# Threshold sums from absolute differences and a key-sum column, and scores in four row tiles, in a sparsemax attention and mixture-of-experts kernel

## The reference

```
x = x + attention(layernorm(x), ctx)        # 16 heads of width 16, 77 keys
x = x + ffn(layernorm(x))                   # top 2 of 8 experts, and one shared expert

scores = (q @ Wq + bq) . (ctx @ Wk + bk) / 4
attn   = max(scores - tau, 0)               # sparsemax: tau such that each row of 77 sums to 1
out    = attn @ (ctx @ Wv + bv);  out @ Wo + bo

hidden = square(relu(x @ w1[e]));  expert = hidden @ w2[e]      # e = 0..7, and the shared one
ffn    = sum over the two picked experts of weight * expert + shared
```

## Time and profile before

| | |
|---|---|
| median of 3 runs | 917.6 us (917.48 to 919.5) |
| the profiled execution | 916.7 us, span 914.9 us, mean granted clock 0.957 |
| busy, share of the span | PE 801.5 us (88%), DVE 593.5 (65%), ACT 571.3 (62%), POOL 538.3 (59%) |
| chain that ended last, by engine | PE 45%, ACT 22%, issue 15%, DVE 9%, POOL 5%, DMA 3% |
| HBM traffic | 36 GB/s over the span |

### The profile page before, as it was taken

How to read it: one execution, slowest core, us unless ns; L and a number is a source line. 1 busy time by engine, 2 the same in 40 slices (tenths; PEclk the granted TensorE clock), 3 DMA queues, 4 the chain that set the end, 5 groups by cost and what they waited for, 6 DMA issues and landing times.

```text
span 914.9 us, 14519 instructions
## 1 busy us (share of the span) xinstructions
PE 801.5 (88%) x4800; PEld 656.7 (72%) x4800; DVE 593.5 (65%) x1691; ACT 571.3 (62%) x890; POOL 538.3 (59%) x622
## 2 busy tenths in 40 slices
PE   1847657999999999999999999999999999889998
PEld 1535435778777777878777877777787877767887
DVE  2469685867676867768586777786777858642221
ACT  1555667676668676767767666867676776633221
POOL 2447586766667584848686666768484858541010
PEclk9977577999999999999999999999999999989999
DMA  8300101020200202020102020110202010101010
GB/s 253 103 8 1 19 12 47 1 73 6 69 3 25 53 12 59 12 64 14 59 1 72 7 70 1 35 43 12 59 13 64 3 59 1 59 1 59 1 58 11
DMA packets 37355, 34.84 MB, mean 38 GB/s; under 512 B 23153, under 2 KB 34078, under 8 KB 35230
## 3 DMA queue, kind: packets, MB, share of 16 engines
q1 hardware_dynamic: 34934, 28.88, 11.3%
q0 software_dynamic: 1248, 4.73, 1.5%
q10 hardware_dynamic: 1096, 0.29, 0.2%
HBM read 28.30 MB, written 4.33 MB: 36 GB/s over the span
## 4 chain that ended last, share of the span: by engine, by line
PE 45%; ACT 22%; issue 15%; DVE 9%; POOL 5%; DMA 3%; ACTq 0%; POOLq 0%; DVEq 0%
PE y_ps L827 18%; PE h_ps L814 11%; ACT signs L533 10%; ACT hid L584 5%; PE m_ps L778 5%; ACT over L535 4%; PE s_ps L769 4%; POOL over L337 3%; DVE fsum L955 3%; PE m_ps L722 3%; DMA sw_all<-sw_scratch 2%; DVE fold_b L961 2%; ACT xn L481 1%; DVE g L1080 1%; PE m_ps L803 1%
## 5 line engine op out<-in xcount | busy, mean ns | idle before, releaser
L337 POOL TENSOR_TENSOR over<-S,tau 128x1232 f32<-128x1232 f32 x128 | 286.6, 2251 | 232.7 <-DVE tau L973 230.1
L827 PE MATMUL y_ps<-w_sb,hid 128*128 128x256 f32 x1152 | 281.5, 388 | 39.9 <-ACT hid L584 30.2
L814 PE MATMUL h_ps<-x1nT,w_sb 128*128 128x256 f32 x1152 | 275.6, 382 | 0.0
L827 PEld LDWEIGHTS y_ps<-w_sb,hid 128*128 128x128 f32 x1152 | 212.8, 191 | 86.1 <-ACT hid L584 57.7
L814 PEld LDWEIGHTS h_ps<-x1nT,w_sb 128*128 128x128 f32 x1152 | 215.2, 191 | 30.4 <-issue 3.0
L955 DVE TENSOR_REDUCE fsum<-over 128x16 f32<-128x1232 f32 x96 | 137.4, 1431 | 40.7 <-ACT over L535 40.6
L535 ACT ACTIVATE over<-over 128x1232 f32<-128x1232 f32 x128 | 155.6, 1228 | 3.0
L584 ACT ACTIVATE hid<-g 128x512 f32<-128x512 f32 x144 | 89.6, 622 | 65.2 <-DVE g L1080 64.7
L1080 DVE SCALAR_TENSOR_TENSOR g<-h_ps,sw_all 128x512 f32<-128x512 f32 x128 | 87.5, 684 | 58.0 <-PE h_ps L814 36.8
L533 ACT ACTIVATE signs<-over 128x1232 bf16<-128x1232 f32 x96 | 117.1, 1220 | 7.4 <-POOL over L337 7.2
L952 DVE TENSOR_TENSOR fold_a<-signs 128x640 bf16<-128x640 bf16 x96 | 55.7, 580 | 47.2 <-ACT signs L533 47.2
(11 more groups left out here) (104 smaller groups left out, 922.4 us busy)
## 6 DMA issues: line engine op xcount, KB each, us to landing
sw_all<-sw_scratch SPq DMA_DIRECT2D x16, 1024.0 KB, 5.2
x_sb<-in_x SPq DMA_DIRECT2D x16, 256.0 KB, 2.7
w_sb<-in_w POOLq DMA_DIRECT2D x2, 2048.0 KB, 12.1
out_y<-wk_sb SPq DMA_DIRECT2D x16, 256.0 KB, 5.6
sw_all<-in_ctx SPq DMA_DIRECT2D x1, 1078.0 KB
v_block<-v_all SPq DMA_DIRECT2D x56, 9.6 KB
wk_sb<-in_wk SPq DMA_DIRECT2D x1, 256.0 KB
wv_sb<-in_wv SPq DMA_DIRECT2D x1, 256.0 KB
```

The costliest lines, as they stand in the source:

```text
L337: return pool.tensor_tensor(dst, S[:, p, t], tau[:, p, t].rearrange("p (h o) -> p h o", o=1).broadcast_to([P, NH, NK]), ALU.subtract)
L814: last = pe.matmul(h_ps[:, i % 2, c, :], w1_sb[:, e, k, c * P:(c + 1) * P], x1nT[:, p, k, :], start=(k == 0), stop=(k == KC - 1))
L827: last = pe.matmul(y_ps[:, t, :], hid[:, i % 2, c, t * P:(t + 1) * P], w2_sb[:, e, c, :], start=(i == 0 and t == 0 and c == 0), stop=(i == ...
```

## The change: what it does

- ACT no longer rectifies `over` in rounds 0 to 2. DVE sums |S − tau| there (`apply_absolute_value`), and 2f = sum of |S − tau| + sum of (S − tau). The second sum is the sum of the row of S less 77 tau (`lean`, one operation on 128x32). The row's sum comes from PE: `kT` gets a 78th column with the sum of the keys (`key_sums`, a DVE reduction for each pair of elements, eight in all, in turns 0 and 1), and so S gets a 78th column. Round 3 and the attention weights still rectify.
- The order in a round of DVE becomes: `fsum` of a tile as soon as `over` is there, then (tile 1) `lean`, then `fold_a`. The tail is `den`, `step`, reciprocal, multiply, add.
- The check marks rows above and rows below (`below`), on DVE (`mid_verdict`, ahead of `g` 8) instead of POOL; PE counts both with two more matmuls per turn.
- The scores take four row tiles of 32 rows with two heads each: eight matmuls of 156 columns, the fourth row tile into bank 0 of `m_ps`; `k_diag` has two heads per row group instead of four. The wait `s_front` goes. The order of heads in S becomes the plain one, so the table `PLACES` goes.

```diff
-HALF = P // 2
-GH = HALF // DH
-PLACES = (0, 1, 2, 3, 14, 15, 4, 5, 6, 7, 12, 13, 8, 9, 10, 11)
+ROWS = 32
+RT = P // ROWS
+GH = ROWS // DH
+KS = NK + 1
+HALF_KEYS = GH * KS
...
-        kT = sb("kT", [P, KC, NB, NK])
-        k_diag = sb("k_diag", [P, KC, GH, NK])
+        kT = sb("kT", [P, KC, NB, KS])
+        k_diag = sb("k_diag", [P, KC, GH, KS])
...
-                pool.wait_ge(k_taken.sem, k_taken.at(b // 2))
+                pool.wait_ge(keys_summed.sem, keys_summed.at(b // 2))
...
-                flat = S[:, p, t].rearrange("p h k -> p (h k)")
-                act.activation(flat[:, 0:12 * NK].rearrange("p (a n) -> p a n", a=2), s_ps[:, 0:2, 0:6 * NK],
+                slots = S[:, p, t].rearrange("p (c r j) k -> p r c (j k)", c=KC, j=GH)
+                act.activation(slots[:, 0:SB], s_ps[:, :, 0:KC * HALF_KEYS].rearrange("p r (c n) -> p r c n", c=KC),
                                ACT.Copy, scale=DH ** -0.5)
-                act.activation(flat[:, 12 * NK:], s_ps[:, 2, 0:4 * NK], ACT.Copy, scale=DH ** -0.5
-                               ).then_inc(s_taken.sem, 1)
+                act.activation(slots[:, SB], m_ps[:, 0, 0:KC * HALF_KEYS].rearrange("p (c n) -> p c n", c=KC),
+                               ACT.Copy, scale=DH ** -0.5).then_inc(s_taken.sem, 1)
...
                     act.activation(signs[:, p, t, :, 0:NK], over[:, p, t], ACT.Sign).then_inc(sign_done.sem, 1)
-                    act.wait_ge(sign_done.sem, sign_done.at(b, rt(r, t)))
-                act.activation(over[:, p, t], over[:, p, t], ACT.Relu).then_inc(relu_done.sem, 1)
+                else:
+                    act.activation(over[:, p, t], over[:, p, t], ACT.Relu).then_inc(relu_done.sem, 1)
...
+                for c in range(KC):
+                    for r in range(RT):
+                        rows = slice(r * ROWS, (r + 1) * ROWS)
+                        bank = s_ps[:, r] if r < SB else m_ps[:, 0]
+                        last = pe.matmul(bank[:, c * HALF_KEYS:(c + 1) * HALF_KEYS], qT[rows, c, t * P:(t + 1) * P],
+                                         k_diag[rows, c].rearrange("p h k -> p (h k)"), start=True, stop=True)
...
+            def key_sums(i):
+                dve.wait_ge(k_taken.sem, k_taken.at(i))
+                dve.tensor_reduce(kT[:, :, 2 * i:2 * i + 2, NK], kT[:, :, 2 * i:2 * i + 2, 0:NK], AX.X, ALU.add
+                                  ).then_inc(keys_summed.sem, 1)
...
+                for t in range(T):
+                    dve.wait_ge(over_ready.sem, over_ready.at(b, rt(r, t)))
+                    dve.tensor_reduce(fsum[:, t * NH:(t + 1) * NH], over[:, p, t], AX.X, ALU.add,
+                                      apply_absolute_value=True).then_inc(f_summed.sem, 1)
+                    if t:
...
+                        dve.scalar_tensor_tensor(lean[:], flat(tau[:, p]), -float(NK), key_totals, ALU.mult, ALU.add
+                                                 ).then_inc(leaned.sem, 1)
+                    elif gap is not None:
+                        gap()
                     dve.wait_ge(sign_done.sem, sign_done.at(b, rt(r, t)))
                     dve.tensor_tensor(fold_a[:, t], signs[:, p, t, :, 0:SW // 2], signs[:, p, t, :, SW // 2:], ALU.add
                                       ).then_inc(signs_folded.sem, 1)
-                    dve.wait_ge(relu_done.sem, relu_done.at(b, rt(r, t)))
-                    dve.tensor_reduce(fsum[:, t * NH:(t + 1) * NH], over[:, p, t], AX.X, ALU.add
-                                      ).then_inc(f_summed.sem, 1)
-                    if gap is not None and t == 0:
-                        gap()
...
                 dve.tensor_reduce(den[:, p], fold_b[:], AX.X, ALU.add).then_inc(newton_chain.sem, 1)
+                dve.wait_ge(f_summed.sem, f_summed.at(b, rt(r, 1)))
+                dve.wait_ge(leaned.sem, leaned.at(b, r + 1))
+                dve.scalar_tensor_tensor(step[:], fsum[:], -2.0, lean[:], ALU.add, ALU.add
+                                         ).then_inc(newton_chain.sem, 1)
                 dve.wait_ge(newton_chain.sem, newton_chain.at(b, n0 + 2))
                 dve.reciprocal(rden[:], den[:, p]).then_inc(newton_chain.sem, 1)
-                dve.wait_ge(newton_chain.sem, newton_chain.at(b, n0 + 3))
-                dve.scalar_tensor_tensor(step[:], fsum[:], -1.0, rden[:], ALU.add, ALU.mult
-                                         ).then_inc(newton_chain.sem, 1)
                 dve.wait_ge(newton_chain.sem, newton_chain.at(b, n0 + 4))
-                dve.scalar_tensor_tensor(flat(tau[:, p]), step[:], 2.0, flat(tau[:, p]), ALU.mult, ALU.add
-                                         ).then_inc(tau_ready.sem, 1)
+                dve.tensor_tensor(step[:], step[:], rden[:], ALU.mult).then_inc(newton_chain.sem, 1)
+                dve.wait_ge(newton_chain.sem, newton_chain.at(b, n0 + 5))
+                dve.tensor_tensor(flat(tau[:, p]), flat(tau[:, p]), step[:], ALU.add).then_inc(tau_ready.sem, 1)
...
+            def mid_verdict(m):
+                dve.wait_ge(attn_ready.sem, attn_ready.at(m))
+                dve.wait_ge(count_done.sem, count_done.at(m - 1))
+                dve.wait_ge(check_chain.sem, check_chain.at(m, 4))
+                dve.scalar_tensor_tensor(unsettled[:], asum[:], -float(NH), tol_sum[:], ALU.add, ALU.is_gt)
+                dve.scalar_tensor_tensor(below[:], asum[:], float(NH), tol_sum[:], ALU.subtract, ALU.is_gt,
+                                         reverse0=True).then_inc(unsettled_known.sem, 1)
...
                 if late:
                     late_weights(b - 2)
+                if mid:
+                    mid_verdict(b - 1)
                 gates(8)
```

More of the change, by code:

```diff
@@ L120, in xattn_moe_kernel @@
         fold_a, fold_b = sb("fold_a", [P, T, NH, SW // 2], BF16), sb("fold_b", [P, T * NH, SW // 4], BF16)
+        lean = sb("lean", [P, T * NH])
         fsum, den = sb("fsum", [P, T * NH]), sb("den", [P, 2, T * NH])
@@ L125, in xattn_moe_kernel @@
         asum, tol_sum, unsettled = (sb(n, [P, T]) for n in ("asum", "tol_sum", "unsettled"))
+        below = sb("below", [P, T])
         unsettled_count = sb("unsettled_count", [1, 1], I32)
@@ L652, in turn @@
                 if new:
[L653 removed]
+                    sign_or_relu(b, p, 1, 0)
                 square(8)
@@ L732, in new_scores @@
                     pe.wait_ge(aT_taken.sem, aT_taken.at(b - 3))
-                for c, r, h0, n, bank, col in ((0, 0, 0, 4, 0, 0), (0, 1, 0, 4, 1, 0), (1, 0, 0, 4, 2, 0),
-                                               (1, 1, 2, 2, 0, 4), (1, 1, 0, 2, 1, 4)):
-                    rows = slice(r * HALF, (r + 1) * HALF)
-                    if (c, bank) == (1, 0):
-                        pe.wait_ge(s_front.sem, s_front.at(b, t + 1))
-                    last = pe.matmul(s_ps[:, bank, col * NK:(col + n) * NK], qT[rows, c, t * P:(t + 1) * P],
-                                     k_diag[rows, c, h0:h0 + n, :].rearrange("p h k -> p (h k)"),
-                                     start=True, stop=True)
-                    if (c, bank) == (0, 0):
-                        last.then_inc(s_front.sem, 1)
+                for c in range(KC):
[4 more added lines that the diff above has]
+                                         k_diag[rows, c].rearrange("p h k -> p (h k)"), start=True, stop=True)
                 last.then_inc(s_done.sem, 1)
@@ L750, in late_unsettled @@
                 pe.wait_ge(y_ready.sem, y_ready.at(m - 2))
-                for t in range(T):
-                    last = pe.matmul(y_ps[0:1, 0, 0:1], unsettled[:, t:t + 1], ones[:], start=(t == 0),
-                                     stop=(t == T - 1))
+                for side in (unsettled, below):
+                    for t in range(T):
+                        last = pe.matmul(y_ps[0:1, 0, 0:1], side[:, t:t + 1], ones[:],
+                                         start=(side is unsettled and t == 0), stop=(side is below and t == T - 1))
                 last.then_inc(count_done.sem, 1)
@@ L928, in new_tau @@
                 for h in range(NH):
-                    last = dve.max(top8[:, t, h], S[:, p, t, h])
+                    last = dve.max(top8[:, t, h], S[:, p, t, h, 0:NK])
                 last.then_inc(top_chain.sem, 1)
```

71 lines of the change are left out of this document (35 added, 36 removed).

## The result

| | before | after |
|---|---|---|
| median | 917.5 us (913.1 to 919.5, 4 runs) | 868.2 us (865.7, 866.9, 869.5; one execution took 4352.1) |
| profiled execution | 916.7, span 914.9 | 865.7, span 863.6, mean granted clock 0.966 |

The ratio is 0.946, with an interval from 0.941 to 0.951: 49 us less, 5.4%. It is formed without the execution of 4352.1 us, which the median of 868.2 still counts (the other three alone have 866.9); that one has a part of its own at the end of the experiments. The predicted 880 lies 12 us above the result, which is inside the predicted range.

What follows compares the result with a forecast made beforehand. PE was taken as near its bound in steady turns, waiting at both ends. Legs of 10.9 + 12.43 + 17.6 + 6.4 make 47.3 us, 27 saved over 13 turns; with 9.5 at the ends, 36.5 saved: 880 us, range 862 to 902.

Steps and rivals of the forecast that it cites:

- (b): PE's leg from layer 2 of expert 2 to the output projection: PE-bound, 12.43 us as before.
- (d): PE's leg from layer 2 of expert 8 to the next layer 2 of expert 0: 7.07 becomes 6.4 us, PE's own work.
- the legs as worked out: The main case, the four legs of a steady turn as priced: 870 to 892 us, chance 0.58.
- rival A: The chains slip away: `lean` misses `xb`, DVE keeps ahead; turn 46.5 us or less, 870 us; chance 0.17.
- (a): PE's leg from layer 2 of expert 0 to layer 2 of expert 2: 12.68 becomes 10.9 us, set by DVE.
- (c): PE's leg from output projection to layer 2 of expert 8: 17.22 becomes 17.6 us, `lean` held by POOL's `xb`.
- The ends: Turns outside the 13 steady ones: shorter rounds gain 10.5 us, 9.5 with the key sums.
- the 1.5 us a round: Gain per round at the ends, from subtraction to `fold_b`, as sign, Relu and sum become sum, `lean` and fold.
- B: Little gain: more DVE-POOL holds (894 us), a costlier reduction, or score tiles not side by side (899 to 914); chance 0.2.
- C: Slower: the recheck fires and DVE repeats steps, about 250 us per element, 1130 us from the first; chance 0.05.

Runs made afterwards that it cites:

- the reordered kernel: On the changed kernel, DVE's statistics of the next element and reading of the count moved ahead of `g` of expert 1; 853.6 us, ratio 0.932.
- the first experiment: The changed kernel with the scores put back on two row tiles of 64 rows, sums, key sums and check as changed; 874.9 us, ratio 0.956.
- the run with them unread: The changed kernel with six Relus a turn put back on ACT, writing a tile that nobody reads; 874.7 us, ratio 0.952.
- the experiment with the old tiles: The changed kernel with two row tiles for the scores and the statistics and count reading moved ahead of `g` of expert 1; 885.1 us, ratio 0.964.

## Why the prediction was right, and where it was off

**The bound and the kind of gain: right.** PE is near its bound in the steady turn, and the legs end where a chain to `hid` ends. Turn: forecast 47.3, measured 46.85 as the mean of turns 3 to 14. **(b)**: forecast 12.43, measured 12.43. **(d)**: forecast 6.4, PE's own time; measured 6.36 to 6.37. The size was off by more than the time suggests: 37 us of gain were forecast, 49 measured. The result lies inside the whole range, but just below the 870 to 892 of the case "the legs as worked out"; the range reached it through rival A. And the turn came within 0.5 us partly by luck, since (a) was forecast 0.5 to 0.8 too short and (c) 0.9 to 1.2 too long.

**The prices.** The absolute sum at the old price: 1427 against 1431 ns. The score block: forecast 0.77, measured 0.75, so column tiles were the right row to read row tiles from. The rule of the Trainium skill (TensorE: Matmul & The Clock Gate, on measured speedup) would have given 0.69; from the estimated 2.13 in a row to 0.75 is 2.8 times, beside its 3.07 for 512 columns. `lean` 0.20 where nothing holds it: right. ACT's turn: forecast 27.5, measured 28.2. DVE's turn: forecast 37.7, measured 36.5.

**(a), forecast 10.9, measured 11.4 to 11.7: right chain, two terms too small.** DVE does set it, and `g` of expert 1 does wait over 1 us for `sw_all` (1.65 in the turn shown). The larger miss is "reading the count and its branch 0.4". I had taken it from a row at 845.19, ahead of a `g` in a turn of the drain, which shows 0.35. Here it costs 0.76 to 1.12, and 0.93 to 1.30 in front of `g` in the reordered kernel. Removing it, or moving it into a wait, brought 12 to 15 us. I should have kept 0.35 as the lower end of a bound. The other is the start of `g` of expert 1, forecast 2.5 into the leg: it comes 2.78 into it in the turn shown (422.41 less 419.63) and 2.5 to 3.1 in the others but one. The rest of the sum holds: statistics 2.30 for 2.3, and from the first sum to PE 5.54 for 5.57, so 2.78 + 2.30 + 1.05 + 5.54 = 11.67. PE alone needs 10.41 where I had 10.8. For the old blocks that reckoning amounts to 12.4, 12.68 less the wait of 0.29, and the first experiment measured 12.07: I hadn't taken off the wait of 0.15 for ACT's copy before the second score block and what goes with it.

**(c), forecast 17.6, measured 16.4 to 16.7: wrong by a mis-timed meeting.** The step that failed is "`xb` ... 7.4 with POOL's chain 0.27 later". `xb` came at 6.71, so `lean`, due at 7.65, met its end only: 0.41 long instead of 1.0 (0.36 to 0.41 in the steady turns). POOL's round 1 then started 11.22 into the leg (454.95 less 443.73), where I had 12.15. The sign that I gave, a wait of PE before layer 2 of expert 8 of over 1 us, didn't come either: it is 0.52. The mechanism is real: the same kind of hold took 0.63 of (c) when the fold ran into `xb`, and moving the fold gave it back. Its place was wrong. The prediction's own figure without the hold was 16.8. The Relus were no cause of (c) beyond 0.34: the run with them unread has 16.75.

**The ends, forecast 9.5, measured about 17.5.** The two sides of the sum, stretch by stretch: before turn 3, 6.5 forecast (five rounds at 1.5, less the key sums) and 12.1 measured; from turn 3 to 15, 12 turns of 2.1, 25, and 31.1 measured; from turn 15 on, 2.1 for that turn and two rounds, 5.1, and 8.1 measured. The mis-sized term is the 1.5 us a round. Round 2 of the first element, from the start of POOL's subtraction to the start of the step that gives the new tau, before and after:

```profile
61.16 4.45 POOL L337 TENSOR_TENSOR over<-S,tau 128x1232 f32<-128x1232 f32 x2 [7.67 <-DVE tau L973]
71.69 0.19 DVE L973 SCALAR_TENSOR_TENSOR tau<-step,tau 128x32 f32<-128x32 f32 x1
```

```profile
53.88 4.46 POOL L342 TENSOR_TENSOR over<-S,tau 128x1232 f32<-128x1232 f32 x2 [5.82 <-DVE tau L977]
62.57 0.19 DVE L977 TENSOR_TENSOR tau<-tau,step 128x32 f32<-128x32 f32 x1
```

That is 10.53 before and 8.69 after, 1.8 less. The five rounds that I counted did shorten the start, as read from the starts of the steps to tau: by 2.0, 2.4, 1.8, 1.6 and 1.8, together 9.6 instead of 7.5; what lies between them gained nothing. Another 2.9 lie ahead of the first subtraction, and most of that is not the change: the first queries' matmuls took 3.78 us in the profile before, 1.99 in the one after, but 3.78 again in the second profile of the kernel after. There the first subtraction starts at 35.00, against 35.25 before and 32.30 in the first profile after. The queries before, and in the second profile after:

```profile
23.63 3.78 PE L722 MATMUL m_ps<-xnT,wq_sb 128*128 128x256 f32 x8 [0.53 <-ACT xnT L508]
```

```profile
23.54 3.78 PE L715 MATMUL m_ps<-xnT,wq_sb 128*128 128x256 f32 x8 [0.53 <-ACT xnT L501]
```

By the second profile turn 3 begins at 141.7, and the start's gain is 10.2. With the sums alone turn 3 already begins at 140.3, so the start's gain is the sums', not the tiles'. Of the tail's 8.1, 3.4 come with the sums alone and 4.7 between that run and the kernel after (166.3 against 161.6). The tiles have at most half of the 4.7: 2.4 lie in the turn from 795.8, in which no scores are computed and which took 43.9 at a granted clock of 0.96, against 41.5 at 1.00.

**The rivals.** A (the chains slip away, 46.5 or less) didn't come about, but half of its reason did: `lean` almost misses `xb`. Its value of 870 is nearer to the result than the forecast, but for another reason: its turns of 46.5 or less didn't come, and the ends gave 17.5 instead of its 10. The kernel with the statistics moved, 45.6 a turn, is what A would look like, 0.5 from the 45.1 that I gave for PE alone. B's tiles in a row are refuted by the blocks of 0.75. B's "a hold of 0.5 more" is in kind what the experiment with the old tiles ran into, in (c) only, at 885. C's price was 250 and is 259; that it fires isn't seen in the trace of the profiled execution.

## What to carry to other kernels

When two parts of a change act on the same leg, neither part's worth is its own: the tiles are worth −17, +8 or, by the estimate above, +22 us, depending on who ends the leg. Ask of each saving which chain is second, and by how much; a saving on PE that becomes PE's idle time can cost clock. And before believing the releaser behind an idle time, see when it ended: if it was done before the idle began and a branch or a register read stands there, look for a wait on the same engine that can cover the branch, and move it there. The move was the cheapest gain of this study, 13 to 15 us without leaving out any work. With the old tiles, where another chain ends the leg, the same move cost 10 us.

## What the hardware showed that I hadn't expected

- Less work on PE made the kernel slower: with the short score blocks and waits of 0.97 and 1.08 us around one of them, the granted clock fell to 0.50 for about 3.4 us in each later turn, 933.7 us against 916.9 with redundant matmuls in the gap. Early turns of the same execution, with the same two waits, kept 1.00.
- Reading a count with its branch costs DVE 0.76 to 1.30 us in a busy turn; the row of the drain had shown 0.35.
- A held bfloat16 fold of two inputs ended 0.34 us behind POOL's instruction; a held `lean` of 128x32 ended 0.08 behind it (451.79 against 451.71). Reductions with one input ran beside `xb` unheld. The Trainium skill (SBUF — State Buffer, on engine-side contention) has the pair taken in turn for whole instructions; both rows agree with it.
